# Row tiles' second norm moved from GpSimd to VectorE, and the second routing group ranked before the list tiles

## The reference

```
x = x + tanh(g0) * softmax(mask((ctx Wq^T + bq)(ctx Wk^T + bk)^T / sqrt(128) * layernorm(x)))
n = layernorm(x)
s = sigmoid(n Wg^T);  top2 of s + bias;  w = s of the two, divided by their sum
x = x + tanh(g1) * sum over the two experts e of
        w_e * (silu(n W1_e^T) * (n W3_e^T)) W2_e^T        (W1_e, W3_e: 256 x 512, W2_e: 512 x 256)
```

## Time and profile before

| | us |
|---|---|
| median of 3 runs | 350.49 (348.11 to 350.96) |
| the profiled execution, whole | 346.8 |
| its span, first to last instruction | 344.9 |
| mean granted TensorE clock | 0.922 of full speed |
| busy: TensorE, VectorE, ScalarE, GpSimd | 286.4, 191.1, 127.8, 195.0 |
| last `nmean` of the row tiles ends | 108.99 |
| first matmul of list tile 0 | 121.02 |

### The profile page before, as it was taken

The page is one execution under the profiler, slowest core; times in us unless marked ns, Lnnn a source line. Parts: engine busy times, 40 slices in busy tenths (PEclk is TensorE's granted clock), DMA queues, the critical chain, the costliest instruction groups (busy, mean ns, idle before and its releaser), DMA issues.

```text
span 344.9 us, 5188 instructions
## 1 busy us (share of the span) xinstructions
PE 286.4 (83%) x1316; PEld 204.4 (59%) x1316; DVE 191.1 (55%) x496; ACT 127.8 (37%) x239; POOL 195.0 (57%) x208
## 2 busy tenths in 40 slices
PE   4889898489876497678776799999999999999981
PEld 1244454245435375565564577888888888888860
DVE  2697868999946287565233325454454454454530
ACT  2678577237626233022122122333323333323320
POOL 5198997266884616616587355635656535664313
PEclk9999899658865599989989999999999999999998
DMA  7999889955833521945669376856666654865345
GB/s 225 331 416 323 269 291 361 291 184 134 158 105 93 141 74 8 62 57 93 63 66 97 30 121 119 130 115 121 114 104 107 115 105 80 153 112 104 56 62 61
DMA packets 27026, 48.69 MB, mean 141 GB/s; under 512 B 9524, under 2 KB 10296, under 8 KB 25976
## 3 DMA queue, kind: packets, MB, share of 16 engines
q0 software_dynamic: 9760, 20.49, 38.6%
q1 hardware_dynamic: 14408, 15.04, 13.6%
q10 hardware_dynamic: 2832, 12.85, 12.3%
HBM read 28.51 MB, written 19.85 MB: 140 GB/s over the span
## 4 chain that ended last, share of the span: by engine, by line
DMA 47%; issue 22%; POOL 12%; DVE 9%; PE 5%; POOLq 2%; ACT 1%; SPq 1%; ACTq 0%; DVEq 0%
DMA out<-rows,slot 29%; DMA out<-rows 8%; POOL rows L439 5%; DMA slot_table<-entry,slot_index 4%; POOL out L458 3%; DMA rows<-in_x 3%; POOL slot_table L426 3%; PE bank L895 2%; DVE rows L691 1%; DVE w_lo L830 1%; POOLq L450 1%; DMA rows<-xn_rows,slot 1%; DMA w_hi<-in_ctx_t 1%; DVE w_hi L668 1%; DVE bn L661 1%
## 5 line engine op out<-in xcount | busy, mean ns | idle before, releaser
L458 POOL DMA_INDIRECT out<-rows,slot x39 | 62.1, 1592 | 75.0 <-DMA out<-rows,slot 37.4
L809 DVE TENSOR_TENSOR xt_lo<-bank,xt_hi 128x512 fp32r<-128x512 f32 x39 | 27.0, 691 | 77.6 <-ACT xt_hi L581 66.3
L984 PE MATMUL bank<-w_hi,xt_hi 128*128 x156 | 65.2, 418 | 0.6 <-issue 0.6
L986 PE MATMUL bank<-w_hi,xt_lo 128*128 x156 | 61.4, 394 | 0.0
L985 PE MATMUL bank<-w_lo,xt_hi 128*128 x156 | 61.4, 393 | 0.0
L602 ACT ACTIVATE rows<-bank,slot 128x512 f32<-128x512 f32 x39 | 26.8, 688 | 73.9 <-DMA out<-rows,slot 40.1
L439 POOL DMA_INDIRECT rows<-xn_rows,slot x39 | 39.2, 1004 | 22.9 <-issue 15.2
L589 ACT ACTIVATE rows<-bank 128x256 f32<-128x256 f32 x39 | 15.0, 385 | 81.2 <-PE bank L986 60.7
L426 POOL DMA_INDIRECT slot_table<-entry,slot_index x32 | 32.9, 1028 | 17.5 <-issue 8.9
L1011 PE MATMUL bank<-w_hi,gt_hi 128*128 x78 | 31.7, 406 | 13.3 <-DVE gt_lo L826 13.3
L815 DVE SCALAR_TENSOR_TENSOR rows<-rows,bank 128x256 f32<-128x256 f32 x39 | 16.3, 418 | 34.5 <-ACT rows L589 32.1
(11 more groups left out here) (128 smaller groups left out, 464.6 us busy)
## 6 DMA issues: line engine op xcount, KB each, us to landing
w_lo<-in_w ACTq DMA_DIRECT2D x8, 1024.0 KB, 7.0
xn_rows<-w_hi SPq DMA_DIRECT2D x17, 256.0 KB, 8.9
rows<-in_x SPq DMA_DIRECT2D x16, 256.0 KB, 4.7
out<-rows SPq DMA_DIRECT2D x16, 256.0 KB, 4.0
w_lo<-in_w ACTq DMA_DIRECT2D x8, 512.0 KB, 5.8
w_hi<-in_ctx_t SPq DMA_DIRECT2D x4, 256.0 KB, 5.4
slot<-slot_table SPq DMA_DIRECT2D x39, 1.0 KB, 2.7
rows<-xn_rows,slot POOLq DMA_INDIRECT x39
```

The costliest lines, as they stand in the source:

```text
L458: pool.indirect_dma_start(out=out[0:SPARE + P * READY[segment(i)], :], out_offset=bass.IndirectOffsetOnAxis(ap=slot[:, i, 0:1].bitcast(U32 ...
L809: dve.tensor_tensor(xt_lo[:, i % 2].rearrange("p k s -> p (k s)"), ps_x[i % 2][:], xt_hi[:, i % 2].rearrange("p k s -> p (k s)").bitcast(F32),
L984: pe.matmul(ps_h[i % 2][:], xt_hi[:, i % 2, k, :], hi, start=(k == 0), stop=False)
L986: mm = pe.matmul(ps_h[i % 2][:], xt_lo[:, i % 2, k, :], hi, start=False, stop=(k == KC - 1))
```

## The change

GpSimd's `normed` becomes VectorE's, and stands there between `score_bias(step)` and the weight splits; the last one stands behind `router_ranks(1)`. In ScalarE's step the copy of the transposed tile comes a step later and ahead of the weight splits; in TensorE's step `logits` comes behind `spin`. The second group's ranks, weights and slots come right behind the last residual instead of within the first list tiles, its positions before the last row tile's transpose, in a bank of their own (`ps_neg`, so they wait for the last `s_zmax`). GpSimd's entries of the first group come one step earlier, those of the second start before list tile 0, those of the third are spread over list tiles 4 to 10. SyncE loads slots 0 to 6 a step earlier. One weight split moves from step 15 to step 14.

```diff
-    SPLITS = (1, 1, 2, 2, 1, 2, 1, 2, 1, 1, 1, 2, 1, 1, 1, 2)
+    SPLITS = (1, 1, 2, 2, 1, 2, 1, 2, 1, 1, 1, 2, 1, 1, 2, 1)
...
-    SCATTERS = {10: (0, 0, 3), 11: (0, 3, 6), 12: (0, 6, 10), 13: (0, 10, 14)}
-    LATE_SCATTERS = {0: (1, 0, 4), 1: (1, 4, 6), 2: (1, 6, 8), 4: (2, 0, 2), 5: (2, 2, 4), 6: (2, 4, 6), 7: (2, 6, 8),
-                     8: (2, 8, 10)}
+    SCATTERS = {9: (0, 0, 3), 10: (0, 3, 6), 11: (0, 6, 10), 12: (0, 10, 14)}
+    LATE_SCATTERS = {0: (1, 6, 8), 4: (2, 0, 2), 5: (2, 2, 3), 6: (2, 3, 5), 7: (2, 5, 6), 8: (2, 6, 8), 9: (2, 8, 9),
+                     10: (2, 9, 10)}
...
@@ SyncE, the steps of the row tiles
-                if step == TILES:
+                if step == TILES - 1:
+                    listed(0)
                     for i in range(4):
                         load_slots(i)
...
@@ GpSimd
-                    normed(step - 1)
                     for unit in units_in(step - 1):
                         if unit in LO_BY_POOL:
                             split_lo(unit)
...
             row_scales(TILES)
-            normed(TILES - 1)
             gather(2)
             gather(3)
+            enter_slots(1, 0, 6)
             for i in range(LIST):
...
@@ ScalarE
                 exponentials(step)
+                if step >= 2:
+                    transposed(step - 2)
+                for unit in units_in(step)[0:2]:
+                    if unit != 2 * E + 4:
+                        split_hi(unit)
...
-                for unit in units_in(step):
-                    split_hi(unit)
                 squares(step)
-                if step >= 1:
-                    transposed(step - 1)
...
@@ VectorE
+            def normed(tile):
+                col = slice(tile % NT, tile % NT + 1)
+                if tile == TILES - 1:
+                    row_done(TILES - 3)
+                elif tile >= 2:
+                    dve.wait_ge(s_xpose, tile - 1)
+                    dve.wait_ge(s_xn_out[tile % 2], 16 * (tile // 2))
+                dve.wait_ge(s_rstd, tile + 4)
+                dve.tensor_scalar(normed_row(tile), x_row(tile), nmean2[:, col], rstds[:, (tile + 3) % NT, 1:2],
+                                   ALU.add, ALU.mult).then_inc(s_xn, 1)
...
                 score_bias(step)
+                if step > 0:
+                    normed(step - 1)
...
-            for unit in units_in(TILES - 1):
+            router_ranks(1)
+            normed(TILES - 1)
+            router_weights(1)
+            gathered_lo(0)
+            router_slots(1)
+            gathered_lo(1)
+            for unit in range(2 * E + 5, UNITS):
                 split_lo(unit)
-            gathered_lo(0)
-            split_lo(UNITS - 2)
-            gathered_lo(1)
-            split_lo(UNITS - 1)
-            router_ranks(1)
...
@@ TensorE
             for step in range(TILES):
-                if step >= 2:
-                    logits(step - 2)
                 if step + 1 < TILES:
                     scores(step + 1)
                     masks(step + 1)
...
                 if step < TILES - 2:
                     spin(projected)
+                if step >= 2:
+                    logits(step - 2)
...
             gathered(0)
+            positions(1)
             transpose(TILES - 1)
```

More of the change, by code:

```diff
@@ L177, in flamingo_routed_block @@
         ps_neg, ps_t, ps_early, ps_q, ps_k, ps_l = bank[2:]
-        ps_pos = (ps_early[:, 0:(MOST + 1) * E],) + 2 * (ps_l[:, 2 * P:2 * P + (MOST + 1) * E],)
+        ps_pos = (ps_early[:, 0:(MOST + 1) * E], ps_neg[:, 0:(MOST + 1) * E], ps_l[:, 2 * P:2 * P + (MOST + 1) * E])
         ps_h = bank[0:2]
@@ L372, in _ @@
                 if step == TILES - 1:
-                    listed(0)
-                elif step == TILES:
                     for i in range(4, FIRST[1]):
@@ L404, in row_done @@
                 pool.wait_ge(s_x1_out[tile % XR], 16 * (tile // XR + 1))
-            def normed(tile):
-                col = slice(tile % NT, tile % NT + 1)
-                if tile == TILES - 1:
-                    row_done(TILES - 3)
-                elif tile >= 2:
-                    pool.wait_ge(s_xpose, tile - 1)
-                    pool.wait_ge(s_xn_out[tile % 2], 16 * (tile // 2))
-                pool.wait_ge(s_rstd, tile + 4)
-                pool.tensor_scalar(normed_row(tile), x_row(tile), nmean2[:, col], rstds[:, (tile + 3) % NT, 1:2],
-                                   ALU.add, ALU.mult).then_inc(s_xn, 1)
             def split_lo(unit):
@@ L631, in _ @@
                     router_tanh(1)
-                for unit in units_in(step):
-                    split_hi(unit)
                 squares(step)
-                if step >= 1:
-                    transposed(step - 1)
+                if step == TILES - 2:
+                    split_hi(2 * E + 4)
                 if step % NT == 2 and step // NT + 1 < B:
@@ L640, in _ @@
                     load_weights(n)
+            transposed(TILES - 2)
             split_hi(UNITS - 2)
@@ L694, in residual, with row_done @@
                 dve.tensor_scalar(nmean2[:, col], sum2[:, col], -1.0 / D, None, ALU.mult).then_inc(s_nmean, 1)
+            def row_done(tile):
+                dve.wait_ge(s_xn, tile + 1)
+                dve.wait_ge(s_x1_out[tile % XR], 16 * (tile // XR + 1))
+            def normed(tile):
[8 more added lines that the diff above has]
+                                   ALU.add, ALU.mult).then_inc(s_xn, 1)
             def rank_step(g, step, instruction):
@@ L872, in _ @@
                     gathered_lo(i + 2)
-                if i == 0:
-                    router_weights(1)
                 gated_transposed(i)
                 if i == 0:
-                    router_slots(1)
-                elif i == 1:
                     list_tiles(1)
@@ L943, in positions @@
                 pe.wait_ge(s_slots, 2 * g)
+                if g == 1:
+                    pe.wait_ge(s_zmax, TILES)
                 pe.matmul(counts, ones[:], chosen_sum[:], start=True, stop=False)
@@ L993, in gate_transpose @@
                 else:
-                    pe.wait_ge(s_zmax, TILES)
+                    pe.wait_ge(s_slots, 4)
                 for c in range(FC):
@@ L1054, in _ @@
                     gate_transpose(0)
-                    positions(1)
                     gathered(3)
```

## The result

The changed kernel takes 357.29 us (median of 4 runs, 356.88 to 358.58), against 349.3 for the kernel before on the same chip (4 runs). The ratio is 1.023, with a 95% interval of 1.017 to 1.029: slower by more than the one percent that a measurement of this kernel can tell. The profiled execution has a span of 355.3 us instead of 344.9, 10.4 longer. The median moved by 8.0.

The account below looks back on a forecast made before the run. Bound by stores and loads in early row tiles, by TensorE from 208 us, with 26.6 us lost between. +21.0 + 2.0 - 4.4 - 12 = +6.6 on 350.49 gives 357.1 us; range 350 to 366.

Parts of the forecast that it names:

- steps 9 to 15: Later row tiles: GpSimd loses its norm, but table entries may hold VectorE's norm; +2.0 us, ends -0.8 and +2.1.
- the hold: Steps 1 to 8: VectorE's norm waits out GpSimd's weight split on the shared port, 8 x 2.35 = 18.8 us more.
- Part 1: Norm moved to VectorE: lengthens steps 1 to 8 by 21.0 us and steps 9 to 15 by 2.0.
- the new wait: Steps 1 to 8: the norm in VectorE's queue waits for the tile's rstd ahead of the next residual; 2.2 us.
- Rival 1: VectorE's norm in steps 1 to 8 is never held by GpSimd's split, about 0.4 us each; 335.5 us, chance 0.30.
- break-even: Mean hold per norm in steps 1 to 8 from which the change is no longer slower: given as about 0.8 us.
- Part 2: New order on ScalarE and TensorE, later transposed copy and logits behind the spinning matmuls: nothing more gained or lost.
- Part 3: Hand-over from last nmean to first list matmul: earlier slot loads and gathers cut 12.0 us to 7.6, gain 4.4.
- Part 4: Second group's table entries first: the list's adds start 9.5 us earlier and 2.6 us go; gain 12, bounds 4 and 20.
- the wait of gather(7) for slots: GpSimd's queue in the list: this wait ahead of add(2) disappears, saving the 2.6 us between 155.42 and 158.03.
- Rival 3: Norm held, and early entries crowd out gathers 4 and 5, so the list gains only 4: +14.6, 365 us, chance 0.06.
- The tail: Later list tiles, where TensorE is full: the pace of 4.79 us a tile should not change.

Follow-up runs that it names:

- e3: Changed kernel, with GpSimd's split made to wait for the norm of its step (one added wait): 341.7 us, ratio 0.982 to the kernel before.
- e10: e3 plus e6's edit, the third group's table entries two by two over list tiles 4 to 8: 336.3 us, ratio 0.969 to the kernel before.
- e9: Kernel before (old order), with the norm on VectorE and each GpSimd split waiting until that norm is done: 350.2 us, ratio 1.008.
- e5: Changed kernel with all expert weight splits on VectorE and none on GpSimd: 348.5 us, ratio 1.002 to the kernel before.
- e1: Changed kernel with the norm back on GpSimd, all else of the new order kept: 338.6 us, ratio 0.972 to the kernel before.
- e6: e1 with the third group's ten table entries laid two by two over list tiles 4 to 8: 338.8 us, ratio 0.966 to the kernel before.
- e7: e1 with the last two table entries of the second group moved from ahead of add(0) to ahead of add(1): 339.6 us, no ratio given.

## Why the prediction was right, and where its terms were not

The forecast was 357.1 us and the median is 357.29, but so close a hit is luck. The predicted sum was +6.6 on the span, the profile shows +10.4. The terms missed by -2.9 (steps 1 to 8), +1.3 (steps 9 to 15), -1.7 (hand-over), +6.1 (list) and +1.0 (the rest), +3.8 in sum. The medians then kept only 8.0 of the 10.4, and the kernel before came out at 349.3 and not at the 350.49 that the forecast started from; these 2.4 and 1.2 us hide the 3.8. What was right is that the hold comes, that it outweighs the gains, and the side on which the kernel ends.

**Part 1, the hold: right mechanism, size 3 us too large.** The forecast was +21.0 for steps 1 to 8, from 2.2 for the new wait and 18.8 for the hold; measured +18.1. The hold itself is 8 x (2.49 - 0.55) = 15.5 us, and e3, which differs from the changed kernel in nothing else, takes 15.6 us less by its median, and 15.9 less for steps 1 to 8 of its profile. The mis-sized step is "2.35 us more" a norm: a held norm does not run its whole length behind the split, it ends 0.28 us after it, and it doesn't start with the split but 0.07 to 0.18 behind. Unheld it takes 0.55 us, not the 0.43 that was taken from the 4x512 row. The wait for rstd, with the norm itself, is left with 18.1 - 15.5 = 2.6 us, against 2.2 in the forecast. How well this is known the profiles without a hold say: steps 1 to 8 took 44.3 us in e3, 47.2 in e10 (the same program there) and 48.0 in e9, against 42.2 before, so 2 to 6 us.

**Rival 1 was decided by the first thing it named.** All eight norms beside a split were held. Its break-even is misstated: by the prediction's own sum the change stops being slower when the mean hold falls by 6.6 / 8 = 0.8 us, to about 1.5, not to 0.8. GpSimd was ahead every time, by 0.07 to 0.18 us; the likely reason, not tried by itself, is that its own next instruction needs no word from another engine.

**Steps 9 to 15: right sum, wrong reason.** The +2.0 was made of entries that hold the norm. None did: the norm is 0.54 to 0.57 beside an entry in the changed kernel, e3, e5 and e9. The +3.3 measured is one profile. Of the other kernels with the new order and the plain norm at the same place, e3 took 52.0, e5 50.7 and e10 50.7, and before the change it was 50.6; e1, e6 and e7, one program there, took 50.6 to 51.6, so 53.9 is more than profiles of one program differ in this stretch. Half of the excess is in step 11, 7.76 us against 6.11 in e3 (L900 are projections, L678 begins the residual):

```profile
98.32 3.62 PE L900 MATMUL bank<-w_hi 128*128 128x512 f32 x4
...
103.49 0.17 DVE L678 RECIPROCAL rden<-prob_sum 128x1 f32<-128x1 f32 x1 [1.52 <-ACT bank L516]
```

The four projection matmuls took 3.62 us, where they took 1.88 in e3; the granted clock in the step was 0.65, in e3 1.00; and VectorE waited 1.52 us for the exponentials behind them, for which it does not wait in e3. Step 15 adds another 1.1 against e5, at a clock of 0.50 against 0.69. The mean granted clock of the changed kernel's four runs is 0.88 to 0.89, that of e10's 0.92 to 0.94; whether the held steps lower the clock, and how much of the time the lower clock then costs, stays open.

**Part 2, nothing for the orders of ScalarE and TensorE:** borne out within the spread. With them and the norm on GpSimd (e1, e6, e7), steps 1 to 8 took 41.2 to 45.9 us against 42.2 before.

**Part 3, the hand-over: -6.1 instead of -4.4.** The chain was 5.9 us and not 7.6, and it is 5.9 in e3, e5 and e10 as well. With the norm on GpSimd it is 7.8 to 10.1 (e1, e6, e7), so the norm on VectorE is worth some 2 us or more in this place, which the prediction did not count. The profiles show where: gather(0) starts 3.3 to 3.5 us ahead of the last nmean's end with the norm on VectorE (the changed kernel, e3, e5, e10), and 0.6 to 3.2 behind it in e1, e6 and e7. Cover that went was no trouble for TensorE: the three splits of 3.49 us ran beside the first matmuls.

**Part 4, the list: -5.9 instead of -12, the real miss.** The prediction let the chain of adds start 9.5 us earlier, as its entries do. (Its own list of signs has add(0) some 13 us behind the first list matmul, which is only 5.7 earlier than the 18.65 before; the sum did not use that.) The entries did start 8.65 us earlier, but add(0) went only 3.4 earlier. Before, GpSimd had six entries and one gather to issue between slot_index and add(0), 9.0 us. Now it is eight entries and two gathers, 14.2 us: ten issues of 1.29 with their gap, and 1.4 for the two entries of 1.37 and 1.96 us that ran beside VectorE's splits (the last section says what holds them). The prediction named gather(4) behind six entries and priced it at nothing. Its other term, the wait of gather(7) for slots, went as it said: add(2) is 6.7 us earlier, of which 4.2 are add(1)'s and 2.5 this wait's. All of that and no more arrives at tile 12 (6.5) and tile 15 (5.9). e7 shows that the missing 2.6 of the last two entries were not to be had by moving them. Rival 3, entries that crowd out what stands behind them, had the mechanism, and the truth lies between it (4) and the forecast (12), nearer to the rival.

**The tail** kept its pace within 1%, 4.79 us a tile against 4.75 over the last 23.

## What to carry to other kernels

Before an operation moves to VectorE to relieve GpSimd, ask what GpSimd will do in the same moment, and in which form VectorE's operation runs. If both are released by one event, GpSimd's next instruction may win by a tenth of a microsecond, as in all eight steps here, and a wait of it on VectorE's operation may be worth more than the move (here 15.6 us for one line). The traces suggest that a hold goes the other way too: GpSimd's norms and table entries ended late beside VectorE's splits (last section). When a group of DMA issues is moved forward in a queue, count all that it is put in front of until the next instruction that somebody waits for, by the issue time of each. An agreeing total is no proof of the terms: only the marks by stage showed which of them were off.
